# One-byte weight inputs for a casting DMA, and normalisation steps moved three slices earlier among the matmuls

## What is computed

```python
xn = layernorm(x)
# recurrent branch, M = 64
q, k, v = xn @ Wq, xn @ Wk, xn @ Wv
g = sigmoid(xn @ Wg + bg)
S = decay * S + (k_t * g_t)[:, :, None] * (v_t * g_t)[:, None, :]   # for each t
s = einsum('bd,bde->be', q_t, S) @ Wo + bo
# FFN branch; w_gate, w_up: int32 [3072, 1024], w_down: int32 [1024, 3072], all in -127..127
gate, up = xn @ (w_gate / 127).T, xn @ (w_up / 127).T
f = (silu(gate) * up) @ (w_down / 127).T
out = x + s * silu(f)
```

## Time and profile before

| | |
|---|---|
| median of 2 runs | 744.69 us (743.77 and 745.6) |
| profiled execution, its own time | 740.75 us |
| its span on the slowest core, core 0 | 739.2 us |
| spans of the eight cores | 731.6 to 739.2 us |
| mean granted TensorE clock | 0.932 to 0.942 |
| PE busy | 610.0 us, 83% of the span |
| DVE, ACT, POOL busy | 36%, 23%, 10% |
| HBM | 89.53 MB read, 8.39 MB written, 132 GB/s over the span |

### The profile page before, as it was taken

How to read it: one execution, slowest core, us unless ns; L and a number is a source line. 1 busy time by engine, 2 the same in 40 slices (tenths; PEclk the granted TensorE clock), 3 DMA queues, 4 the chain that set the end, 5 groups by cost and what they waited for, 6 DMA issues and landing times.

```text
span 739.2 us, 8535 instructions; the slowest of 8 cores (731.6 to 739.2 us)
## 1 busy us (share of the span) xinstructions
PE 610.0 (83%) x2996; PEld 289.7 (39%) x2996; DVE 265.6 (36%) x477; ACT 169.1 (23%) x268; POOL 73.3 (10%) x146
## 2 busy tenths in 40 slices
PE   0442957757977559899889999899999999999997
PEld 0310423324544324355334444344444444444443
DVE  2457152654856752426332212211221211212222
ACT  0532043363455320202100101011111111100100
POOL 4000101112112002001100000011111111000000
PEclk9965989878989869999999999999999999999999
DMA  9840548356555509313312233154544554112232
GB/s 169 150 72 1 70 73 127 58 86 103 92 91 89 98 0 151 50 29 58 58 29 55 88 114 109 63 112 66 80 76 73 80 85 65 23 57 72 100 113 86
DMA packets 24747, 58.63 MB, mean 79 GB/s; under 512 B 2753, under 2 KB 2881, under 8 KB 24706
## 3 DMA queue, kind: packets, MB, share of 16 engines
q0 software_dynamic: 19584, 39.85, 35.1%
q1 hardware_dynamic: 4608, 16.78, 6.5%
q10 hardware_dynamic: 514, 1.45, 0.7%
HBM read 89.53 MB, written 8.39 MB: 132 GB/s over the span
## 4 chain that ended last, share of the span: by engine, by line
PE 70%; DVE 10%; DMA 8%; issue 7%; ACT 3%; POOL 1%; ACTq 0%; DVEq 0%; POOLq 0%
PE pb L712 40%; PE pb L783 23%; DMA xstage<-xpfm 4%; DVE abig L394 3%; DMA xstage<-xfm 2%; PE pb L506 2%; DVE xn L398 1%; ACT xsqf L307 1%; DVE wd_bf L398 1%; DMA abig<-wob 1%; DMA bgs_s<-bgs 1%; PE pb L799 1%; PE pb L539 1%; PE pb L423 1%; ACT vtmp L363 1%
## 5 line engine op out<-in xcount | busy, mean ns | idle before, releaser
L712 PE MATMUL pb<-xn,gubf 128*128 128x512 bf16 x1536 | 356.8, 393 | 49.1 <-DVE xn L398 28.2
L712 PEld LDWEIGHTS pb<-xn,gubf 128*128 128x128 bf16 x1536 | 152.8, 101 | 240.0 <-issue 78.3
L783 PE MATMUL pb<-wd_bf,h_bf 128*128 128x512 bf16 x768 | 170.4, 382 | 1.4 <-DVE h_bf L739 1.4
L739 DVE SCALAR_TENSOR_TENSOR h_bf<-pb,sgbf 128x512 bf16<-128x512 f32 x96 | 66.2, 690 | 272.5 <-PE pb L712 210.1
L734 ACT ACTIVATE sgbf<-pb 128x512 bf16<-128x512 f32 x96 | 56.7, 592 | 271.7 <-PE pb L712 267.1
L783 PEld LDWEIGHTS pb<-wd_bf,h_bf 128*128 128x128 bf16 x768 | 75.3, 98 | 93.5 <-issue 4.2
L679 POOL DMA_DIRECT2D gubf<-wgu x96 | 51.0, 538 | 492.0 <-PE pb L712 417.4
L826 DVE TENSOR_TENSOR abig<-abig,pb 128x512 f32<-128x512 f32 x32 | 22.0, 687 | 131.5 <-DMA xtmt<-xtm 67.4
L817 ACT ACTIVATE abig<-pb 128x512 f32<-128x512 f32 x32 | 19.1, 597 | 162.6 <-PE pb L783 162.6
L307 ACT ACTIVATE xsqf<-xstage 128x1024 bf16<-128x1024 bf16 x32 | 31.9, 1046 | 91.7 <-DMA xstage<-xpfm 45.6
L158 ACT ACT_TABLE_LOAD x32 | 41.1, 1283 | 0.6
(11 more groups left out here) (85 smaller groups left out, 207.1 us busy)
## 6 DMA issues: line engine op xcount, KB each, us to landing
gubf<-wgu POOLq DMA_DIRECT2D x96, 256.0 KB, 4.9
xtmt<-xtm SPq DMA_DIRECT2D x16, 512.0 KB, 4.1
out<-xtmt SPq DMA_DIRECT2D x16, 512.0 KB, 2.9
wd_bf<-wdt POOLq DMA_DIRECT2D x24, 256.0 KB, 7.9
xstage<-xfm POOLq DMA_DIRECT2D x8, 512.0 KB, 9.6
xstage<-xpfm POOLq DMA_DIRECT2D x8, 512.0 KB, 9.1
abig<-wqk ACTq DMA_DIRECT2D x1, 512.0 KB
xtmt<-wkvg ACTq DMA_DIRECT2D x1, 512.0 KB
```

Of the source, the lines that this page charges most:

```text
L712: e.matmul(out=o, lhsT=gu_bf[gpar][:, gu * 1024 + dc * 128: gu * 1024 + (dc + 1) * 128], rhs=xn[:, dc * N + half * 1024 + nh * 512: dc * N ...
L739: e.scalar_tensor_tensor(out=h_bf[:, hc * 1024 + nh * 512: hc * 1024 + nh * 512 + 512], in0=a, scalar=QS, in1=sg_bf[:, sgp * 512:(sgp + 1) ...
L783: e.matmul(out=o[:, dh * 512:(dh + 1) * 512], lhsT=h_bf[:, hc * 1024 + nc2 * 128: hc * 1024 + (nc2 + 1) * 128], rhs=wd_bf[:, hc * 1024 + d ...
```

## The change

The host hands over the lowest byte of each weight (they lie within -127 to 127), and `wgu` and `wdt` are int8 tensors; the DMAs cast int8 to bf16. `lnA_c` is followed by two down loads where there was one. And `take` is 2 from E(1) on, where it was 1 for the first six slices.

```diff
-    wgu = nc.dram_tensor("wgu", [NHC, 128, 2048], I32, kind="ExternalInput").ap()
-    wdt = nc.dram_tensor("wdt", [NHC, 128, 1024], I32, kind="ExternalInput").ap()
+    wgu = nc.dram_tensor("wgu", [NHC, 128, 2048], I8, kind="ExternalInput").ap()
+    wdt = nc.dram_tensor("wdt", [NHC, 128, 1024], I8, kind="ExternalInput").ap()
...
-                pre.append(lambda ti=k - 1: (lnA_c(ti), emit_wd_loads(1)))
+                pre.append(lambda ti=k - 1: (lnA_c(ti), emit_wd_loads(2)))
...
-            take = (1 if fi < 6 else 2) if pi < len(pre) else 0
+            take = 2 if pi < len(pre) else 0
...
+    def low_bytes(a):
+        a = np.ascontiguousarray(np.asarray(a, np.int32))
+        return np.ascontiguousarray(a.view(np.int8).reshape(*a.shape, 4)[..., 0])
+
+    wg_i = low_bytes(L0_ffn_w_gate)
+    wu_i = low_bytes(L0_ffn_w_up)
+    wd_i = low_bytes(L0_ffn_w_down)
```

More of the change, by code:

```diff
@@ L11 @@
 I32 = mybir.dt.int32
+I8 = mybir.dt.int8
 AF = mybir.ActivationFunctionType
@@ L938, in make_in_maps @@
     dp = np.asarray(L0_attn_decay_param, f32)
-    wg_i = np.asarray(L0_ffn_w_gate, np.int32)
-    wu_i = np.asarray(L0_ffn_w_up, np.int32)
-    wd_i = np.asarray(L0_ffn_w_down, np.int32)
+    def low_bytes(a):
[4 more added lines that the diff above has]
+    wd_i = low_bytes(L0_ffn_w_down)
     wqk_c = np.concatenate([Wq, Wk], axis=1)
```

## The result

The changed kernel takes 697.53 us at the median against 743.44, a ratio of 0.9383 with a 95% interval of 0.9362 to 0.9405: 46 us less. The forecast was 705, the range 691 to 722. The profiled execution took 698.45 us; its slowest core, core 7, spans 696.9, so against the profiled execution of before it is 42.3 us shorter.

The account below looks back on a forecast made before the run. It took a loop of waits around each tile's load, not an engine, to bound the first stage; O(3) at 109.5, plus 87.1, 29.0 and 10.4, gave 236.0 against 275.4, so 701.4, and 705.3 at the median, range 691 to 722 us.

Parts of the forecast that it names:

- main case: Whole kernel: tiles paced by a three-chunk passage and cheaper int8 loads, about 699 to 711 us; chance 0.66.
- better: First token half: tiles run at PE's floor, 3 x 8.7 + 5 x 10.5, 8.5 us less, 697 us; chance 0.12.
- offset: Whole kernel: median of two runs lies 3.94 us above the profiled execution, added to 701.4 to give 705.3.
- eight chunks to the end of O(11): First token half after O(3): three own tiles at 10.7 us and five of the other half at 11.0, 87.1 us.
- tail to the last projection: After O(11), to the end of tile 15's projection: 29.0 us, from 29.8 before, ending at 225.6.
- one weight load: POOL's DMA queue: a load cast from one byte takes 1.0 us where the four-byte one took 1.72.
- PE's floor: PE's lower limit per tile: 8.7 us, and 10.5 with the projection of about 1.8 us.
- The stages behind: Projections and recurrence, 275 to 389 us before, then the rest: steps for each slice kept, change costed at 0.
- the walk: From O(0)'s end at 76.6 us through tile 5's load, landing at 86.8, to O(3)'s end at 109.5.
- two-chunk wait: Tile passage stays two chunks, 14.2 us a tile: 732 us, no measurable change; chance 0.06.
- The byte buys nothing: Weight loads stay at 1.72 us, in the walk and six chunks: some 9 us more, 714 us; chance 0.12.
- dear cast: One-byte cast costs more, deciding from 3.46 us a load: 745 us, or 784 at 4.0; slower, chance 0.04.

Follow-up runs that it names:

- advances of one and two slices: Changed kernel with take 1 for the first four slices (steps one slice earlier than before): 702.86 us; for the first two (two slices earlier): 726.37 us.
- early load: Kernel before, int32 and old order, each tile's load from tile 5 issued with the squares of the tile before: 688.38 us; same edit in changed kernel: 686.60 us.
- the kernel that does it: Kernel before with take 2 from E(1) and two down loads a tile, weights left int32: 713.59 us, ratio 0.9609.

## Why the prediction was right

**The mechanism** was shown, not only fitted. The tile's uncovered landing set the pace; the change stretches its passage from two chunks to three. The advances of one and two slices show that the phase does it. The early load takes the landing out of PE's waits and leaves the queues of PE, ACT and DVE in their order; in the old order it brings more than the whole gain, and with it order and bytes are nearly indifferent.

**The number owes something to luck.** The time of 697.5 lies below the 699 to 711 of my main case and on the 697 of the *better* one, but not by that one's reason: its eight chunks would take 78.6 us and took 85.4. Of the 7.8 us between 705.3 and 697.5, 4.9 are the offset below, which has nothing to do with the change.

**The terms of the sum**, predicted and measured:

| term | forecast | measured |
|---|---|---|
| start of O(0) | 70.2 | 69.95 |
| end of O(3) | 109.5 | 109.4 |
| eight chunks to the end of O(11) | 87.1 | 85.4 |
| tail to the last projection | 29.0 | 26.5 |
| last projection | 225.6 | 221.3 |
| from there to the down projection, bare slices taken off | 114.0 (as before) | 117.1 |
| one weight load | 1.0 | 0.85 |

- **Eight chunks.** The term that was mis-sized is PE's floor: I took the projection of a tile for 1.8 us. The row at 142.59 has the 16 matmuls in 1.07 us, 0.91 from start to start. PE's floor for these tiles is 9.6 us and not 10.5, and I had rounded up because of it. Five chunks came at 10.4 us each (forecast 11.0). The three own ones came at 11.1, over my 10.7, since I took the slice behind the stop at full clock, 3.46 us, where the row at 132.25 has 5.30; in the walk I had priced the same slice at 5.12. The passage from 109.4 took 33.3 us to the end of O(6) where I had 31.2; its other terms came within 0.3 us each.
- **The tail**, 2.5 us too long in my sum: ahead of the projections of the last tile but one PE stood 1.67 and 1.89 us, where I had carried over the old stretch with its stops of 3.33 and 2.04; the slice behind them took 4.66 us and not 5.61.
- **The stages behind**, costed at 0, lost 3.1 us: 348.8 - 221.3 - 10.4 against 389.4 - 275.4. The slice behind the last projection ran slowly for longer, 5.6 us against 4.4, and the down projection waits 1.37 us for the product of the last slice, which used to be covered by steps of the recurrence. I had named no cover there. The down projection behind it gave 1.7 us back: to the next slice it takes 88.95 us where it took 90.63, with its first matmuls at full clock behind the bare slices (15 in 3.40 us), where before the first 18 took 5.73.
- **The offset** of 3.94 us between the profiled execution and the median came from two executions. With eight the kernel before has 743.44, 2.7 over its profiled execution, and the changed one lies 0.9 below its own. That is 4.9 us of the distance; the other 2.9 us are the sum, which was that much too long.

**The rivals.** The two-chunk wait was real, but belongs to an advance of two slices (726 us, forecast 732 on int32 prices). *The byte buys nothing* was priced at 9 us over the forecast; the kernel that does it took 16 over the changed one. Its trace shows the step that failed there, the walk to O(3). O(0) starts at 71.62, 1.7 us later than in the changed kernel, and the first tile is squared 15.7 us after POOL's issue (78.17 to 93.87) against 9.7 (76.72 to 86.40): 6 us more where I had 2.9. E(3) starts 7.5 us later, at 106.21; from there to the last projection it loses 6.6 us, near the 6 that I had priced for the chunks. Why the loads in the walk took longer than their prices add up to isn't shown. The dear cast didn't show: it is half the old price. The better case assumed PE's floor of 8.7 and 10.5; with the early load most tiles come at 9.4 and 9.9.

**What I had said would show it.** The share fell to 22.2% (forecast 25), the three bare slices are there, the stage of 768 matmuls didn't change, and the last projection ended in the window named. Three signs were put too strictly: the loads don't come evenly, since a passage of three chunks leaves one long wait in three; ACT waited 6 to 8 us for some tiles, not under 5; and PE's clock from 110 to 240 us was 0.93, not near 1.00, since the stops stayed.

**A rule weighed.** By the fit of the Trainium skill, "DMA: Bandwidth & Descriptors", Anatomy of one DMA, a one-byte load would take, as an estimate on the bytes written, 0.6 us beyond the fixed time. The trace doesn't agree: it has 0.85. The rows of plain transfers, halved, had 0.75 and were nearer. With the fixed 2.0 us of the Trainium skill's fit that estimate is 2.6 us from issue to landing, and the trace's median is 2.8.

## What to carry to other kernels

When a chain of waits contains a transfer, ask first what its issue stands behind, before making the transfer or what is queued ahead of it smaller: one queue entry moved by a round was worth more here (55 us) than a new order and weights of a quarter of the bytes together (46 us). Where two lists are interleaved, the phase between them can matter more than how far one is ahead, and a step of one slice can gain what a step of two loses. Slices that run bare at the end of a stage are cover that can be spent where an engine waits, and are best placed last, by the rows of its waits.

## What the runs showed of the hardware

In time of all 16 DMA engines, a POOL DMA that casts one byte to two costs 0.85 us for 0.13 MB read and 0.26 MB written, one that casts four bytes to two 1.72 us for 0.52 MB read and again 0.26 MB written, and a plain one of 0.52 MB, from SyncE's queue, 1.51 us. So the larger of the two sides comes near to setting the price, 0.26 and 0.52 MB at 0.30 to 0.35 MB a us, and the number of elements, the same for both casts, doesn't. The two casts alone would fit the sum of both sides as well (0.39 and 0.79 MB at 0.46 MB a us); only the plain transfer speaks against that, with 1.05 MB at 0.69. A busy queue cost the engines little: with the early load in the old order, tiles of the other half came every 9.9 us with int32 weights, but for one of 11.6, and with int8 alike, though the DMA share from 110 to 240 us was 0.79 in the one and 0.49 in the other.
